# A batched four-layer transformer block kernel: the stack is loaded in two halves by heads, each with its own signal, and the transpose of maxima stands behind the fourth plain score pair

## The reference

```
h = modulate(norm(x));  q, k, v = split(h @ w_qkv + b)      # 16 heads of 9 features
a = softmax(q @ k.T / 3);  x = x + gate * ((a @ v) @ w_o + b_o)
h = modulate(norm(x));     x = x + gate * (gelu(h @ w1 + b1) @ w2 + b2)   # 576 hidden
```

## Time and profile before

| what | value |
|---|---|
| three runs, us | 1487.57, 1484.27, 1486.37; median 1486.37 |
| profiled execution | 1485.1 us, of which the span is 1483.4 us |
| PE, DVE, ACT, POOL busy | 85%, 76%, 63%, 22% of the span |
| mean granted TensorE clock | 0.956 of full speed |
| chain that ended last, by engine | PE 36%, DVE 20%, DMA 12%, ACT 11%, issue 11%, SPq 6% |
| first issue of the stack load, bodies 2, 3 and 4 | 250.78, 299.55, 346.70 us |
| the same in layer 1 | 699.81, 736.52, 773.15 us |
| the same in layer 3 | 1155.02, 1198.16, 1238.79, 1281.22 us |

### The profile page before, as it was taken

The page is one execution under the profiler, slowest core; times in us unless marked ns, Lnnn a source line. Parts: engine busy times, 40 slices in busy tenths (PEclk is TensorE's granted clock), DMA queues, the critical chain, the costliest instruction groups (busy, mean ns, idle before and its releaser), DMA issues.

```text
span 1483.4 us, 36868 instructions
## 1 busy us (share of the span) xinstructions
PE 1256.1 (85%) x13282; PEld 808.8 (55%) x13314; DVE 1121.3 (76%) x2839; ACT 935.5 (63%) x2107; POOL 325.4 (22%) x446
## 2 busy tenths in 40 slices
PE   6365779888869999999999999999878898888886
PEld 4122335655446666666666666666645565656654
DVE  3844668877778888888888888888868888897642
ACT  0032456657637777777777777777657777776763
POOL 2000111111122222222222222222233343333301
PEclk9996688999979999999999999999989999999998
DMA  6304444234424444444444454444599999999900
GB/s 183 102 0 105 114 107 111 74 72 120 115 75 116 126 128 126 126 125 127 124 125 126 125 127 124 126 124 126 122 94 130 96 124 137 143 136 114 89 26 24
DMA packets 198481, 163.63 MB, mean 110 GB/s; under 512 B 80136, under 2 KB 182480, under 8 KB 192160
## 3 DMA queue, kind: packets, MB, share of 16 engines
q1 hardware_dynamic: 189920, 153.60, 54.5%
q10 hardware_dynamic: 8384, 7.69, 1.8%
HBM read 98.05 MB, written 62.41 MB: 108 GB/s over the span
## 4 chain that ended last, share of the span: by engine, by line
PE 36%; DVE 20%; DMA 12%; ACT 11%; issue 11%; SPq 6%; ACTq 3%; another core or an unknown queue 0%; DVEq 0%; POOL 0%; POOLq 0%
PE lin L1515 7%; PE lin L1531 6%; DMA norm_room<-stack_dram 5%; DMA stack_room<-stack_dram 4%; DVE maxima L1120 4%; PE o_bank L1468 4%; ACT hT_last L713 3%; PE score_bank L1406 3%; ACT p_room L732 3%; PE score_bank L1362 2%; PE st_bank L1437 2%; ACT h2T L718 2%; ACT h1T L718 2%; DVE gated L1178 2%; SPq L421 2%
## 5 line engine op out<-in xcount | busy, mean ns | idle before, releaser
L1120 DVE TENSOR_REDUCE maxima<-score_bank 128x4 f32<-128x512 f32 x512 | 329.1, 684 | 109.1 <-PE score_bank L1406 107.6
L732 ACT ACTIVATE p_room<-st_bank 128x512 f32<-128x512 f32 x512 | 276.9, 598 | 117.5 <-PE st_bank L1437 87.9
L616 POOL TENSOR_TENSOR part_low<-qk_rest,part_mid 96x512 bf16<-96x512 f32 x96 | 111.2, 1158 | 405.5 <-DVE part_mid L1103 405.5
L1531 PE MATMUL lin<-w_f,gelu 128*128 128x144 f32 (+1 forms) x1280 | 181.2, 299 | 3.8 <-ACT max_T L815 2.5
L1531 PEld LDWEIGHTS lin<-w_f,gelu 128*128 128x128 f32 (+1 forms) x1280 | 171.6, 201 | 7.3 <-ACT max_T L815 3.7
L1515 PE MATMUL lin<-h2T,w_h 128*128 128x512 f32 (+1 forms) x320 | 170.6, 632 | 4.4 <-ACT h2T L718 2.6
L1406 PE MATMUL score_bank<-stack_room 62*128 62x128 bf16 x2048 | 104.5, 223 | 77.3 <-DMA stack_room<-stack_dram 34.1
L1468 PE MATMUL o_bank<-p_room,v_room 128*32 128x128 f32 x4096 | 168.0, 282 | 0.4 <-issue 0.4
L607 POOL TENSOR_TENSOR x<-x,gated 128x288 f32<-128x288 f32 x64 | 53.9, 843 | 417.7 <-DVE gated L1178 417.7
L848 ACT ACTIVATE gelu<-lin 128x512 f32<-128x512 f32 (+1 forms) x160 | 90.9, 589 | 83.3 <-PE lin L1519 76.5
L1406 PEld LDWEIGHTS score_bank<-stack_room 62*128 62x128 bf16 x2048 | 59.8, 96 | 149.7 <-issue 47.2
(11 more groups left out here) (194 smaller groups left out, 2434.7 us busy)
## 6 DMA issues: line engine op xcount, KB each, us to landing
stack_room<-stack_dram SPq DMA_DIRECT2D x96, 512.0 KB, 8.4
stack_dram<-part_high SPq DMA_DIRECT2D x64, 288.0 KB
gates<-gates_dram SPq DMA_DIRECT2D x64, 288.0 KB, 3.3
norm_room<-stack_dram SPq DMA_DIRECT2D x32, 512.0 KB, 9.6
stack_dram<-part_mid SPq DMA_DIRECT2D x64, 192.0 KB
stack_dram<-part_high SPq DMA_DIRECT2D x64, 144.0 KB
stack_dram<-part_mid SPq DMA_DIRECT2D x64, 96.0 KB
stack_dram<-part_low SPq DMA_DIRECT2D x64, 96.0 KB
```

The source lines that it names most:

```text
L616: eng.tensor_tensor(part_low[:, T, :], qk_rest[:, T, :], part_mid[:, T, :], ALU.subtract)\
L732: eng.activation(probs[:, i % PBUFS, :], st_bank[i % 2][:, :], ACT.Exp, scale=float(HD) ** -0.5)\
L1120: eng.tensor_reduce(maxima[:, b, CH * c:CH * c + CH], bank_of(f"S{i}")[:, :].rearrange("p (h k) -> p h k", h=CH), AX_X, ALU.max)\
L1531: ins = eng.matmul(o, gelu[0:k, T, b * TOK:(b + 1) * TOK], w_f2[l][0:k, T, :], start=T == 0, stop=T == FCT - 1)
```

## The change

The stack load of a group is eight DMAs instead of four. The first four carry, for q and k and both halves of the partitions, the first four heads of each partition half (chunks 0 and 2) and signal `stack_loaded`; the next four carry the others (chunks 1 and 3) and signal the new `stack_rest_loaded`. In flow "a" a run is 4 KB instead of 8 KB. In flow "t" the halves are by heads too (0 to 7, 8 to 15), in pieces of 512 bytes as before. `scores` waits for the first signal at pair 0 and for the second at pair 1 (flow "a"). Every other reader of the stack or of `stage` waits for both.

The transpose of maxima `flip_max(J, 0)` stands behind `scores(J, 3)` instead of ahead of it; in `late` bodies the order is as before.

```diff
@@ uses_of @@
-    order += [("mT0", J)] + ([] if late else scores[3]) + [("OD1", g)] + (scores[3] if late else [])
+    order += ([] if late else scores[3]) + [("mT0", J), ("OD1", g)] + (scores[3] if late else [])
@@ SP: store_parts, mask_on, load_max (b == 0); POOL: order_keys; ACT, DVE: order_queries @@
                 need(eng, "stack_loaded", ..., STACK_LOADS - 1)
+                need(eng, "stack_rest_loaded", ..., STACK_LOADS - 1)
@@ SP: load_stack @@
-                    for s in range(2):
-                        for f in range(2):
-                            eng.dma_start(stack[L % 2][s][f * HALF:(f + 1) * HALF, :],
-                                          stack_dram[L % 2][s, :, f * HEADS // 2:(f + 1) * HEADS // 2, :]
-                                          .rearrange("r h n -> r (h n)")).then_inc(S["stack_loaded"], 16)
+
+                    n = HEADS // 4
+                    for k, loaded in enumerate(("stack_loaded", "stack_rest_loaded")):
+                        for s in range(2):
+                            for f in range(2):
+                                at = f * HEADS // 2 + k * n
+                                eng.dma_start(stack[L % 2][s][f * HALF:(f + 1) * HALF, k * n * GT:(k + 1) * n * GT],
+                                              stack_dram[L % 2][s, :, at:at + n, :].rearrange("r h n -> r (h n)"))\
+                                   .then_inc(S[loaded], 16)
...
-                for s in range(2):
-                    for f in range(2):
-                        eng.dma_start(stage[s][f * HALF:(f + 1) * HALF, :].rearrange("r (h n) -> r h n", h=HEADS),
-                                      stack_dram[L % 2][s, :, :, f * GT // 2:(f + 1) * GT // 2])\
-                           .then_inc(S["stack_loaded"], 16)
+                n = HEADS // 2
+                for k, loaded in enumerate(("stack_loaded", "stack_rest_loaded")):
+                    for s in range(2):
+                        for f in range(2):
+                            rows = stage[s][f * HALF:(f + 1) * HALF, :].rearrange("r (h n) -> r h n", h=HEADS)
+                            eng.dma_start(rows[:, k * n:(k + 1) * n, :],
+                                          stack_dram[L % 2][s, :, k * n:(k + 1) * n, f * GT // 2:(f + 1) * GT // 2])\
+                               .then_inc(S[loaded], 16)
@@ PE: scores @@
-                elif pair == 0:
-                    need(eng, "stack_loaded", g, STACK_LOADS - 1)
+                elif flow_of(g) == "a" and pair < 2:
+                    need(eng, ("stack_loaded", "stack_rest_loaded")[pair], g, STACK_LOADS - 1)
@@ PE: body @@
-                flip_max(J, 0)
                 if not late:
                     scores(J, 3)
+                flip_max(J, 0)
```

More of the change, by code:

```diff
@@ L173 @@
 }
-PER_GROUP_DMA = {"parts_stored": 4 * 3, "stack_loaded": STACK_LOADS, "m_loaded0": 2, "m_loaded1": 2, "m_loaded2": 2,
+PER_GROUP_DMA = {"parts_stored": 4 * 3, "stack_loaded": STACK_LOADS, "stack_rest_loaded": STACK_LOADS, "m_loaded0": 2, "m_loaded1": 2, "m_loaded2": 2,
                  "m_loaded3": 2, "gates0_loaded": 1, "gates1_loaded": 1,
@@ L407, in store_parts @@
                         need(eng, "stack_loaded", L - 2, STACK_LOADS - 1)
+                        need(eng, "stack_rest_loaded", L - 2, STACK_LOADS - 1)
                     for s, T, p0, p1 in ((0, 0, 0, QKM), (0, 1, 0, DIM - QKM), (1, 1, DIM - QKM, QKM), (1, 2, 0, QKM)):
@@ L486, in load_max @@
                     need(eng, "stack_loaded", g, STACK_LOADS - 1)
+                    need(eng, "stack_rest_loaded", g, STACK_LOADS - 1)
                 for f in range(2):
```

## The result

| what | before | after |
|---|---|---|
| runs in one comparison, us | 1479.63 to 1487.57, median 1485.32 (4) | 1427.93 to 1436.99, median 1431.94 (4) |
| profiled execution, us | 1485.1, span 1483.4 | 1427.93, span 1426.2 |

The ratio is 0.9648, 95% interval 0.9606 to 0.969.

What follows compares the result with a forecast made beforehand. PE was busy 85% of the 1483.4 us span, the rest waits. Gains of 22.4 (layer 0), 13.1 (layers 1 and 2) and 3.6 (layer 3), 39.1 in all, gave 1446.0, as median 1447.3; range 1435 to 1466.

Steps and rivals of the forecast that it cites:

- Halves in the order of issue, `scores(J, 0)` free at half the load: Layer 0, body 3: first half lands at 307.2, so the first scores start at 307.3 instead of 312.0, 4.7 us earlier.
- part 1: Stack load in halves with two signals: 22.4 us gained in layer 0, 0 in the other layers.
- The last of eight at 312.0, as now: Layer 0, body 3: the eighth load lands no sooner than the last of the four old ones.
- the maxima 0.4 us behind it: Layer 0: maxima of sequence 2 land 0.4 us after the last load, bounds 0 and 1.7; the shifted scores wait for them.
- The clock given back, 1.16 us: Layer 0: without PE's stand `down(Q,0)` keeps its clock; scores to shifted scores take 3.95 us instead of 5.11.
- Part 2 in layers 1 and 2, 0.82 by 16: Transpose of maxima behind the fourth pair: 0.82 us gained in each of 16 bodies, 13.1 us.
- Rival 1: The moved transpose gives little, 0 to 7.3 us, as the ring closes elsewhere: 1457 to 1464 us; chance 0.12.
- In layer 3 a half gives nothing: Layer 3: every reader waits for both halves and the load is limited by data, so gain 0.
- +2 us a load: Layer 3: upper bound on the cost of four more issues, for 7 loads; expected 0.
- 3.6 predicted: Layer 3: gain from the moved transpose, 0.6 us in each of 6 bodies; the true step may be 0 or 1.
- Rivals 2 and 3: 2: eight loads land together near 312, halves give nothing, 1470, chance 0.08. 3: serial cost per load, slower, chance 0.04.
- Rival 5: Whole kernel: more than forecast, as waits further down close up as well, below 1435 us; chance 0.03.

Runs made afterwards that it cites:

- e4: Changed kernel with its eight loads, but pair 0 waits for both signals and the transpose of maxima is in its old place: 1465.93 us, ratio 0.9895.
- e7: Changed kernel, layers 0 to 2 loading 32 rows in 8 KB runs, pair 0 waiting for all eight, transpose in its old place: 1463.81 us, ratio 0.9878.
- e2: Kernel before with only the transpose of maxima moved behind the fourth pair, four whole stack loads kept: 1469.31 us, ratio 0.9926.
- e12: The kernel before, unchanged, run once more for the scatter of its layer 3 periods: 1476.94 us, ratio 0.9999.
- e1: Changed kernel with the transpose of maxima back in its old place, load still in halves: 1446.81 us, ratio 0.9774 to the kernel before.
- e3: Changed kernel, but layer 3 loads its stack in four whole loads on one signal: 1441.09 us, ratio 0.9729 to the kernel before.
- e11: The changed kernel, run once more for the scatter of layer 3: 1431.15 us, ratio 0.9685 to the kernel before.
- e9: Kernel before, with useless matmuls added while PE stands for the stack load in layer 0: 1480.35 us, ratio 1.001.
- e5: Changed kernel with sixteen stack loads of 128 KB a group, eight to a signal: 1445.58 us, ratio 0.9739 to the kernel before.
- e8: Changed kernel, each half in layers 0 to 2 being two 512 KB loads over all 128 partitions: 2094.61 us, ratio 1.4135 to the kernel before.
- e10: Changed kernel, with useless matmuls added in PE's remaining waits in bodies -1 and 0: 1429.5 us, ratio 0.9677 to the kernel before.

## Why the prediction was right and wrong, point by point

- **Halves in the order of issue, `scores(J, 0)` free at half the load**: right. The half was there 7.24 us after the first issue in body 3 (7.6 predicted), 7.2 to 8.6 in layer 0, and e4 shows the price of doing without: about 19 us of part 1.
- **"The last of eight at 312.0, as now", with the maxima 0.4 us behind it**: wrong, and the failed step of layer 0. In body 3 the eight land 0.8 us sooner, on average over layer 0 0.6 sooner (11.8 us after the first issue in four kernels with eight loads, 12.4 in three with four). And the maxima don't land behind them: the shifted scores that wait for them go 11.62 us after the first issue in body 3, with the last load in at 11.62, and 11.28 in body 0, with the last load in at 11.72. The prediction had 12.85. In bodies 0 and 1 PE waits for exactly those maxima (1.33 and 1.38 us), and body -1 starts `scores(0, 1)` 11.2 us after the first issue, not 12.3, so there the step is passed on. e7 shows that the smaller load, not the run, does it. The gains by body, in the pair of profiles above and as means (before, e2 and e12 against after, e1, e3 and e11, whose code in layer 0 is the same):

| body | -1 | 0 | 1 | 2 | 3 | 4 | 5 | sum |
|---|---|---|---|---|---|---|---|---|
| predicted, us | 2.1 | 1.3 | 1.3 | 4.1 | 4.7 | 4.45 | 4.45 | 22.4 |
| the pair | 3.2 | 2.9 | 2.4 | 4.6 | 6.1 | 5.2 | 4.6 | 28.9 |
| means | 3.5 | 2.4 | 1.8 | 4.7 | 5.4 | 5.5 | 3.9 | 27.3 |

  One period scatters by up to 3 us among kernels with the same code, so the means are the better reading. Bodies -1, 0, 1 and 3, where a later landing held PE in the forecast, make 3.8 of the 4.9 us that the means have too much.
- **The clock given back, 1.16 us**: right kind, too small; e9 measures 1.63 in body 3. In bodies 2, 4 and 5, where PE waits for no load any more, the missing 0.5 each fits the sum of the means (14.1 against 13.0), but not body by body (5.5 and 3.9 where 4.45 was forecast); that part is argued, not shown.
- **Part 2 in layers 1 and 2, 0.82 by 16**: right, 0.84 a period; 14.6 us, because 17 periods are shorter, not 16, the first of them by 1.7 (e2 has 13.9). Rival 1 is refuted.
- **"In layer 3 a half gives nothing"**: wrong, and the other failed step. It is true that no reader uses the half. But the load is in the chain, and its end moved about 0.67 us a group, 4.7 us; the table has 5.7 to 7.8. What the rest comes from isn't settled: several engines share that chain. The prediction's bound, +2 us a load, looked at the wrong side only. With the order's 1 to 3 us (3.6 predicted) the stage gains 9.0 by the means (415.7 to 406.7), 5.4 more than forecast; what the pair of profiles has above that, 11.4, is scatter.
- **2.3 us ahead of the first load** are scatter: the kernel before started its first load at 118.6 in e12, at 120.45 in its own profile. So the 53 us also have luck in them; on e11's chip the gain is 47.5 (1478.67 to 1431.15), on either reading above 39. The means of the stages add up to 27.3 + 14.6 + 9.0 = 50.9.
- **Rivals 2 and 3**: a load has no serial cost that adds up. Eight loads end sooner than four. A cost appears only where the issue on SP is the limit: e5. The Trainium skill ("DMA: Bandwidth & Descriptors", "Rules for kernel authors") says of two transfers to disjoint partition halves "Don't bother — they serialize"; its fit with the fixed 2 us is for DMAs issued from GpSimd, and these are issued from SyncE. That the loads serialize, the traces agree (1.12 us apart). That the cut isn't worth it, they don't: e7 cuts just so in layers 0 to 2, 32 of 64 partitions each, and is 17.6 us faster than the kernel before without using a half.
- **Rival 5**, below 1435, at 0.03, is where the time came out, but not by its mechanism: no wait further down was found to close up; the load itself landed sooner, and the clock was worth more.

## What to carry to other kernels

Where a reader waits for a queue of large loads, cut them until the issue becomes the limit: here 0.6 us of issue against 1.1 us of data a load at eight, and a loss of some 12 to 14 us at sixteen. Give the first-used part its own signal, and cost both effects apart, the earlier half and the earlier end. When a transfer is on the chain, "same bytes" doesn't mean "same landing"; ask for both signs of its bound. A stand of PE can cost more than its length, here 1.6 us on top of 4.7: price the slower clock of everything between the stand and the next wait. And where a stage scatters by several us between profiles of one kernel, as layer 3 does here, average several kernels that share it before explaining a difference.

## What was not expected of the hardware

- DMAs of 512 KB with an outermost dimension of 2 ran at 52 GB/s, where those with the 64 rows outermost had 205 (e8 and the earlier trace rows).
- SP's issue time goes with the rows: 0.6 us for 64 rows, whether 4 or 8 KB each, 0.44 for 32 rows (e7).
- In body 3 a load of 128 KB landed 3.0 to 3.5 us after its issue (e5), the first of eight of 256 KB 3.8 (after), the first of four of 512 KB 5.3 (before).
- Filling a stand with work that nobody needs kept the granted clock at 1.00 behind it, where it had been 0.57 (e9, body 3) and 0.50 (e10, body -1, shorter by 2.9 us). In e4 the clock was up again in time for body -1's `spread_norms` without such work, the only one of the 12 profiles without it where it was.
